# A second sign tile in the convolutions of a wavelet-attention and binary-convolution block, with the next image's signs written one piece per output copy

## The reference

```
x = x + L0(_gn(x))      # wavelet query, 3x3 key and value, attention over channels, projection
x = x + L1(_gn(x))      # two binary convolutions, each with a batch norm

def L1(x):
    out = conv3x3(sign(x),   sign(w1) * mean|w1|);  out = batchnorm(out)   # over all 4 images
    out = conv3x3(sign(out), sign(w2) * mean|w2|);  out = batchnorm(out)
    return out + x
```

## Time and profile before

| | |
|---|---|
| median of 3 runs | 1374.42 us (1373.09 to 1375.93) |
| the profiled execution, its own time | 1371.92 us |
| its span in the trace | 1370.0 us |
| block of the convolutions | 906 to 1370 us |
| first convolution, image 0 to 3 | 947 to 1147 us |
| second convolution | 1155 to 1298 us |
| output | 1305 to 1370 us |
| busy in the whole span | TensorE 86%, VectorE 75%, ScalarE 65%, GpSimd 32% |

### The profile page before, as it was taken

The page is one execution under the profiler, slowest core; times in us unless marked ns, Lnnn a source line. Parts: engine busy times, 40 slices in busy tenths (PEclk is TensorE's granted clock), DMA queues, the critical chain, the costliest instruction groups (busy, mean ns, idle before and its releaser), DMA issues. The chain is left out here.

```text
span 1370.0 us, 33894 instructions
## 1 busy us (share of the span) xinstructions
PE 1182.8 (86%) x12758; PEld 929.9 (68%) x12758; DVE 1025.6 (75%) x1771; ACT 889.5 (65%) x1574; POOL 433.7 (32%) x476
## 2 busy tenths in 40 slices
PE   0997989999999999999999999748999997999900
PEld 0553658999999999999999999414555554555500
DVE  6776547999999999999999999258666643163494
ACT  0666887888888889888889886013244255766382
POOL 6200034555565655656556554100000010000010
PEclk9999988999999999999999999869999999999955
DMA  9997872544544535534534532386775230000079
GB/s 331 418 268 284 298 266 75 138 102 129 135 109 130 149 94 134 146 94 134 147 101 126 150 104 74 126 350 223 261 257 184 77 121 0 1 0 0 0 309 398
DMA packets 146919, 220.71 MB, mean 161 GB/s; under 512 B 115000, under 2 KB 116196, under 8 KB 142176
## 3 DMA queue, kind: packets, MB, share of 16 engines
q1 hardware_dynamic: 135696, 151.97, 36.9%
q0 software_dynamic: 6480, 47.19, 9.0%
q10 hardware_dynamic: 4608, 19.67, 3.6%
HBM read 131.58 MB, written 86.93 MB: 159 GB/s over the span
## 5 line engine op out<-in xcount | busy, mean ns | idle before, releaser
L1761 PE MATMUL b_conv_bank<-b_sign,wsign 128*128 (+1 forms) x1728 | 297.6, 329 | 10.3 <-ACT b_sign L1537 7.7
L1761 PEld LDWEIGHTS b_conv_bank<-b_sign,wsign 128*128 128x128 bf16 x1728 | 168.9, 98 | 142.2 <-issue 29.9
L824 POOL TENSOR_TENSOR b_vacc<-b_vacc 128x576 f32<-128x576 f32 x128 | 180.4, 1410 | 195.0 <-ACT b_vacc L919 194.2
L1060 PE MATMUL b_bank<-b_tkh,x_first 96*96 96x100 f16 x1536 | 220.9, 210 | 2.4 <-DVE b_tml L1041 2.4
L1062 PE MATMUL b_bank<-b_tkh,x_first 96*96 96x100 f16 x1536 | 220.7, 210 | 0.0
L1061 PE MATMUL b_bank<-b_tkl,x_first 96*96 96x100 f16 x1536 | 220.6, 210 | 0.0
L1060 PE MATMUL b_bank<-x_first,b_tmh 96*96 96x200 f16 x768 | 195.1, 254 | 15.0 <-DVE b_yl L1025 10.0
L1018 DVE SCALAR_TENSOR_TENSOR b_value_sum<-b_vin,value_taps,b_value_sum 128x576 f32<-128x576 f32 x256 | 206.6, 807 | 0.0
L1060 PEld LDWEIGHTS b_bank<-b_tkh,x_first 96*96 96x96 f16 x1536 | 193.2, 126 | 4.0 <-DVE b_tml L1041 2.7
L1062 PE MATMUL b_bank<-x_first,b_tml 96*96 96x200 f16 x768 | 193.6, 252 | 0.0
L1062 PEld LDWEIGHTS b_bank<-b_tkh,x_first 96*96 96x96 f16 x1536 | 193.2, 126 | 0.0
(11 more groups left out here) (230 smaller groups left out, 2688.2 us busy)
## 6 DMA issues: line engine op xcount, KB each, us to landing
b_vin<-value_projection_scratch SPq DMA_DIRECT2D x32, 686.0 KB, 5.8
keys_scratch<-b_khl SPq DMA_DIRECT2D x24, 784.0 KB, 4.7
value_projection_scratch<-b_vout ACTq DMA_DIRECT2D x24, 784.0 KB, 5.4
x_first<-keys_scratch SPq DMA_DIRECT2D x128, 147.0 KB, 3.0
x_first<-in_x SPq DMA_DIRECT2D x128, 144.0 KB, 5.3
values_scratch<-b_vacc SPq DMA_DIRECT2D x32, 576.0 KB, 3.4
out<-xs SPq DMA_DIRECT2D x25, 576.0 KB, 6.7
b_x<-in_x POOLq DMA_DIRECT2D x9, 1536.0 KB, 19.8
```

The lines of the kernel that those rows point to most:

```text
L824: nc.gpsimd.tensor_tensor(whole, whole, room, ALU.add).then_inc(s_padd, 1)
L1060: nc.tensor.matmul(out, w_hi, m_hi, start=first, stop=False)
L1761: ins = nc.tensor.matmul(cbank[k % NBK][:, 0:CH].rearrange("p (r c) -> p r c", c=W), p["wsign"][nth // NIMG][:, t * C:(t + 1) * C], padded ...
```

## The change

A second padded sign image, `sg2`, is laid over the memory of `back`, which is empty until the x1 pieces come back. Images 0 and 2 of the first convolution take `sg2`, all others `sg`. The signs of images 1 to 3 now wait only for the convolution of two images before. GpSimd zeroes the pads of both tiles, ScalarE waits for all eight memsets, and the x1 pieces come back only when the convolution of image 2 is done. At the three turns, ScalarE writes one sign piece behind each of the copies 19 to 23, where it wrote two, and the other seven pieces behind them.

```
+        sg2 = back[:].rearrange("p a n -> p (a n)").bitcast(BF16)[:, 0:PADN]
...
+        def signs_of(nth):
+
+            return padded(sg2 if nth in (0, 2) else sg[:])
+
...
-            for k in (0, WP - 1):
-                nc.gpsimd.memset(sg[:, k * WP:(k + 1) * WP], 0.0).then_inc(s_z, 1)
-                nc.gpsimd.memset(padded(sg[:])[:, 1:WP - 1, k:k + 1], 0.0).then_inc(s_z, 1)
+            for t in (sg2, sg[:]):
+                for k in (0, WP - 1):
+                    nc.gpsimd.memset(t[:, k * WP:(k + 1) * WP], 0.0).then_inc(s_z, 1)
+                    nc.gpsimd.memset(padded(t)[:, 1:WP - 1, k:k + 1], 0.0).then_inc(s_z, 1)
...
             pool.wait_ge(s_pm, NIMG * NCH)
+            pool.wait_ge(s_cm, (NIMG - 1) * NCH)
...
-            act.wait_ge(s_z, 4)
+            act.wait_ge(s_z, 8)
...
-                if nth:
-                    act.wait_ge(s_cm, (nth - 1) * NCH + min(NCH, ((r + 1) * NR + 1) // ROWS + 1))
-                nc.scalar.activation(padded(sg[:])[:, 1 + r * NR:1 + (r + 1) * NR, 1:1 + W],
+                old = nth - 2 if nth < NIMG else nth - 1
+                if old >= 0:
+                    act.wait_ge(s_cm, old * NCH + min(NCH, ((r + 1) * NR + 1) // ROWS + 1))
+                nc.scalar.activation(signs_of(nth)[:, 1 + r * NR:1 + (r + 1) * NR, 1:1 + W],
...
-                        for r in range(2 * (k - last - 1), 2 * (k - last)):
-                            x1_sign(b + 1, r)
+                        x1_sign(b + 1, k - last - 1)
                 if b + 1 < NIMG:
-                    for r in range(2 * (RC - 1), NP):
+                    for r in range(RC - 1, NP):
                         x1_sign(b + 1, r)
...
-                                           padded(sg[:])[:, ds(r * (RC * ROWS) + (k * ROWS + t // 3), ROWS), t % 3:t % 3 + W],
+                                           signs_of(nth)[:, ds(r * (RC * ROWS) + (k * ROWS + t // 3), ROWS), t % 3:t % 3 + W],
```

## The result

The changed kernel took 1362.86 us, the median of 6 runs (1360.04 to 1365.80), against 1372.86 for the kernel before, run beside it: a ratio of 0.9927, 95% interval 0.9906 to 0.9949. That is 10 us less, outside the stated range (1366.0 to 1372.7) by 3 us. The same kernel was timed twice more, 12 runs each, and gave 0.9975 (0.9957 to 0.9992) and 0.9971 (0.9953 to 0.9990). The first interval overlaps neither of these. So the size of the gain has to be read from the traces, by stage.

A forecast was written before the change was run, and what follows sets the result against it. TensorE was taken as busiest, idling at image turns behind ScalarE's signs and late copies. First two turns 4.8 less third turn 0.4 gave 4.4 us: 1374.42 to 1370.0 us, range 1366.0 to 1372.7.

The forecast's parts named there:

- First turn: Image 1's start: copy 23 on time, 2.60 us TensorE idle gone, clock stays up; 4.7 us gained, 2.95 if it falls.
- Second turn: Image 2's start: the add for image 3 waits for x until about 1050.4; both turns together gain 4.8 us.
- x's landing: Last piece of image 3's x at the second turn: landing at 1049.2, or 1050.3 with the added memsets.
- VectorE's want: Second turn: VectorE ready for its first add of image 3 at 1047.6, from 1055.23 less 7.65.
- the memsets' 1.1: Four more GpSimd memsets: 1.0 to 1.1 us, carried through the row of transfers to x of image 3; bounds 0 and 1.1.
- the rival: Second turn: x isn't what it waits for, as transfers go faster; gain 8.4 us, 1366.0 us; chance 0.17.
- the full gain: Both first turns gain in full: 4.7 + 2.95 + 1.15 - 0.4 = 8.4 us, 1366.0; chance 0.17.
- the hold: Second turn: x of image 3 holds VectorE's add; the forecast case, a gain of 2.8 to 6.5 us, chance 0.57.
- Third turn: Image 3's start: ScalarE's row up to image 3's first copy ends 0.3 to 0.4 us later; TensorE idles once, about 3.3 us.
- the clock's 1.6 us: Third turn: the TensorE clock's fall costs 1.6 us now and was kept, with 0 and twice that as bounds.
- The second tile: Second sign tile: its looser waits free nothing, and the x1 pieces' later return has 200 us of cover; costs nothing.
- The reading over the whole span: Improve the engine with highest occupancy, TensorE, first; this change then gains nothing, 1374.4 us; no effect had chance 0.05.

The follow-up runs named there:

- x later: The changed kernel with eighteen memsets of an unused tile, each waited for, ahead of image 3's x loads; ratio to the kernel before 1.0087.
- before again: The kernel before, unedited, run once more against itself for a second trace; ratio 1.0018 (1.0002 to 1.0035).
- tile only: The changed kernel with two sign pieces behind each copy put back, keeping the second sign tile; ratio to the kernel before 0.9990.
- pace only: The kernel before with one sign tile, but one sign piece behind each of the copies 19 to 23; ratio to the kernel before 0.9945.
- x in pairs: "pace only" with the last six sign pieces between the next image's first copies and image 3's x loads issued in pairs; ratio to the kernel before 0.9928.

## Why the prediction was wrong

**First turn, forecast 4.7 us: right.** 56.19 became 51.75 in all three traces, 4.4 us; copy 23, the vanished idle time and the clock all as stated. Both halves were there: TensorE's wait, and the fall of its clock behind it.

**Second turn: the step that failed.** I forecast both turns together at 4.8, so 0.1 for this one. It gave 3.8 in two of three traces and 2.5 in the third, where x did hold the add by 1.17 us. I had put x's landing at 1050.3 and VectorE's want at 1047.6, x late by 2.7. In the profile after, x was 1.7 early. Of these 4.4 us to be explained, measured from image 0's aggregate, 3.1 are the landing, which came after 106.2 us and not 109.3. In them is the memsets' 1.1, which I carried to the end of the row of transfers and which doesn't show there; the rest is scatter: the same distance is 103.0 in the second trace of the full change, 109.2 in the third, and 108.2 and 105.5 in the two of before. The other 1.3 are the want, which came later: 1.0 because the stretch "to turn 1" was longer, 0.3 because the first turn gave less. Counted from the start of the block, where the row of transfers begins, the landing is only 1.6 early (142.3 us, I had 143.9) and the want 2.8 late (143.9, I had 141.2); the split depends on the origin, the 4.4 don't.

The transfers beside the turns were not faster, as the rival would have it: from the first store of x1 of image 1 to the last landing they took 59.0 us in the profile after and 55.5 in the one of before. The row was ahead already at that store, 83.3 us behind the start of the block against 87.3, before anything of the new order at the turns had run, and the second and third trace of the full change have 83.7 and 87.7 there. The mechanism exists, since "x later" costs 15 us by it.

What failed is a slack taken from one trace: by the second trace of before (8.6 us) the same sum, 8.6 - 7.65 - 1.1, has x late by 0.1 and not by 2.7. One trace couldn't tell a slack of -2.7 from one of +1.7, and the full gain should have had as much chance as the hold, not 0.17 against 0.57. That rival (8.4 us, 1366.0) is the one that came true by stage, and even it lies above the first median.

**Third turn, forecast a loss of 0.4: right in kind, too small on average.** ScalarE's row from its first sign to its first copy of image 3 is 0.4 longer (11.8 for 11.4) and TensorE's one wait 3.3 to 3.4. Against 48.67 the loss is 0.1 to 0.5, against the second trace's 47.28 it is 1.5 to 1.9, in the mean 1.1. I had kept the clock's 1.6 us on both sides. In the two-piece order TensorE's clock fell behind the wait of 2.13 us in one trace of three (before, but not before again nor "tile only"); with one piece behind each copy it fell behind the wait of 3.3 to 3.4 us in all three traces of the full change and in "pace only".

**The second tile, worth nothing: right**, by two experiments.

**The sum.** 4.4 + 3.8 - 0.5 gives 7.7 between the first two traces, against 4.4 forecast. What I had not in the sum is "to turn 1": 46.8 in both traces of before and 47.8 to 47.9 in the three of the full change, a loss of 1.0 to 1.1. It is the half clock at the start of the first convolution, which lasts longer in these. From the aggregate at 941.01 on in the trace of before, and from the one at 938.33 on in the one after:

```profile
941.00:943.00 2.00, 1.07 (x5) 0.80 (x6) 1.27 (x4) 0.33 (x1) 0.18 (x1) 1.00 0.00 0
...
939.00:941.00 2.00, 1.75 (x4) 1.26 (x5) 0.77 (x5) 0.81 (x1) 0.53 (x1) 0.50 0.17 74
941.00:943.00 2.00, 2.00 (x4) 1.01 (x3) 1.48 (x3) 2.00 (x4) 0.00 (x0) 0.50 0.96 401
```

Before, TensorE has 1.00 for two more microseconds and then 0.50 for three to four; after, it has 0.50 for more than 6. But "pace only" and "x in pairs", which are the kernel before up to there, took 47.8 and 48.0, and "x later", which is the full change up to there, took 46.8. So both programs give both values, and it isn't shown that the loss is the change's. With it the traces give 4.4 + 3.4 - 1.1 - 1.1 = 5.6 us in the mean, without it 6.7. The other 4.4 of the first 10 us aren't in these stages. I put them down to the scatter of whole executions (the start of the block alone lies 4.2 apart in the first pair), but most of the runs behind the first ratio have no trace, so that isn't shown. The two later ratios, some 3.4 and 4.0 us, lie 1.6 to 2.2 below that mean. That they come near the forecast of 4.4 is luck: the turns did not add up to it in the way I had it. What makes the block start up to 7 us apart stays open.

The reading over the whole span that I weighed from the Trainium skill (Perfetto Trace Analysis, Identifying the Most-Contended Engine) falls: ScalarE had 65% occupancy and TensorE 86%, and reordering ScalarE's work alone made the gain.

## What to carry to other kernels

Where an engine has both a copy that frees a bank and other work to do, count them per round of the engine that it feeds: one sign and one copy (1.20 us) fit beside a chunk of 1.47, two signs and a copy (2.03) don't, and the surplus shows up as someone else's wait. Spread such work over both sides of a turn, ahead of it as much as fits and the rest between the next copies, before reaching for a second buffer. And when a forecast rests on a slack of a few us against a row of chained transfers, give both outcomes real weight: such a row scattered by 6 us in 140.

## What the runs showed of the hardware that I had not expected

A row of twenty chained transfers on GpSimd's queue, in five traces with nearly the same work around it, ended anywhere from 103.0 to 109.2 us behind image 0's aggregate, or 139.2 to 145.5 behind the start of the block. Whether TensorE's clock falls behind a wait differed from place to place and once from trace to trace. Behind 2.60 us of idle time at the first and at the second turn it was granted 1.2 GHz for over 3 us in all three traces of the two-piece order. Behind 0.95 and 1.27 us of waiting at the second turn it kept 2.4 GHz, the wait cost only 1.3 and 1.6 us of the turn, and the next three projections took 3.01 and 3.02 us (3.75 to 3.90 behind the longer wait). Behind 2.13 us at the third turn it fell in one trace and not in two.
